# The down product of a feed-forward block by Strassen-Winograd instead of directly, in an attention and feed-forward kernel on one core

## Chip, core and metric

One of the eight cores of a Trainium2 chip. The metric is device time in microseconds of one execution, the median of several. The kernel is written with one program per engine and semaphores between them: TensorE (matmuls), VectorE, ScalarE, GpSimd, and SyncE, which issues every DMA. Each program runs in its written order.

## What is computed

`x` has 2 x 512 tokens of 1024 features. Three layers (a quantized product, a stream mixer, a cross-attention) come first; they are not touched. The last layer is a feed-forward block with low-rank corrections:

```python
gate = x @ gate_w.T + (x @ gate_a.T) @ gate_b.T      # 1024 -> 2752, rank 16
up   = x @ up_w.T   + (x @ up_a.T) @ up_b.T
hidden = silu(gate) * up
out = hidden @ down_w.T + (hidden @ down_a.T) @ down_b.T   # 2752 -> 1024
x = x + out
```

## The kernel before

Every float32 matrix is held as a float16 high half and a float16 low half (value minus high half), and a product is three matmuls: high x high, high x low, low x high. Splitting costs one ScalarE operation (the high half, a copy) and one VectorE operation (the low half, a subtraction). Weights are staged in four slots `STAGE` of 128 x 1024 float32; TensorE forms the rank-16 correction of a weight block in PSUM ("fold", contraction over 96 partitions), and VectorE adds it to the staged weights.

**Up stage.** Hidden features go in 21 slabs of 128 (`j` = 0 to 20) and a tail of 64 (`TAIL` = 21). Gate and up weights of a slab, and the tokens in two halves, form a 2 x 2 block matrix product that is already done by Strassen-Winograd: seven products A11, A12, S1, S2, S4, S3, A22 (`BLOCKS`) of 4 contraction tiles x 3 = 12 matmuls of 128x512 each. `form` makes S1 to S4 of the staged weights, `block_hi` and `block_lo` split them into a ring of 12 blocks (`SLAB`), `product` (line 2518 issues its matmuls) runs in the order of `products(j)`: S1, S2, S4 of slab j, A11 of j+1, S3 of j, A12 of j+1, A22 of j. `gate_second`, `up_second`, `gate_first` and `keep_*` combine the products; `hidden_second` and `hidden_first` multiply silu(gate) by up for the two token halves; `hidden_hi` and `hidden_rest` split the result into `HIDT` (hidden features x tokens). Some buffers of one slab lie in the place of a later slab of `HIDT` (`kept`, `silu_of`).

SyncE loads slab weights one by one (line 547): each load waits until the low half that last reads its slot is written. VectorE's loop over `j` (lines 2104 to 2137) and ScalarE's (lines 1294 to 1310) are written out by hand; both do slab j's sums, slab j+1's blocks and the first blocks of slab j+2.

**Down stage.** Output features are eight rows `m` of 128. For each m, `down` takes all 21 full hidden tiles x 2 token halves x 3 matmuls (`mm3`, lines 2170 to 2172), and two matmuls for the tail tile (lines 2574, 2575), into `PAIR[m % 2]`. The weights of a row come in pieces of 8, 8, 5 and half a hidden tile (`PIECES`), each folded (`down_fold`, line 2550), added (`down_add`, 1759) and split (`down_hi`, `down_lo`) into one of two buffers `DWN`, a row ahead. The residual x, of which four tiles were spilled to `x_keep` in the up stage, is read back, split into halves (`residual_hi`, `residual_lo`), transposed by DMA and summed into `OUT` (`residual_sum`); `finish` adds the scaled product (line 1789), and `send` stores it. Last, `out_t` (transposed) leaves with 2 KB rows.

Of the kernel before, what the change touches and what calls it, by code (L numbers as in the profile page):

```python
# [5 lines left out]
P = 128  # L6
B, S, D = 2, 512, 1024
# [45 lines left out]
N_LOADS = N_DOWN + KD * NP  # L53
ZEROED = 8 + N_DOWN - N_DF
# [37 lines left out]
def products(j):  # L92
# [7 lines left out]
         + [(TAIL, "L3"), (TAIL, "L4")])  # L100
# [45 lines left out]
def build(nc, x, ctx, ctx_t, consts, small_w, w_branch, wq, wk, bqk, gate_w, up_w, tail_w,  # L146
          down_w, down_tail, gate_a, gate_bt, up_a, up_bt, down_a, down_bt, out_t, x_keep):
    stack = ExitStack()
    with stack:
# [50 lines left out]
        DWN = [SLAB[:, at * KB:at * KB + 2 * HT * P].rearrange("p (s k c) -> p s k c", s=2, k=HT) for at in (0, 13)]  # L200
        XR = XT[:, :, :, :, :].rearrange("p b s k t -> p (b s k t)").rearrange("p (g s d) -> p g s d", g=NT, s=2)
# [5 lines left out]
        XD = X[:, :, :].rearrange("p g d -> p (g d)").bitcast(F16).rearrange("p (s m t) -> p s m t", m=KD, s=2)  # L207
# [54 lines left out]
        DA, DB = LORA[:, D:D + HID], LORA[:, 0:D]  # L262
# [8 lines left out]
        def factors_of(g, si, sj):  # L271
# [26 lines left out]
        out_done, spilled, xd_ok = [sem("out_even"), sem("out_odd")], sem("spilled"), sem("xd_ok")  # L298
# [14 lines left out]
        fac_ok, s_add, comb, b_lo, d_add, d_lo, xr_lo, out_v = (  # L313
            sem(n) for n in ("fac_ok", "s_add", "comb", "b_lo", "d_add", "d_lo", "xr_lo", "out_v"))
# [11 lines left out]
        b_hi, sg_ok, hid_hi, p1_ok, p5_ok, p6_ok, d_hi, xr_hi = (  # L326
            sem(n) for n in ("b_hi", "sg_ok", "hid_hi", "p1_ok", "p5_ok", "p6_ok", "d_hi", "xr_hi"))
# [8 lines left out]
        fold_p, mul_p, dfold_p, down_p = (sem(n) for n in ("fold_p", "mul_p", "dfold_p", "down_p"))  # L336
# [101 lines left out]
        def block_source(j, name):  # L438

            st = [STAGE[(N_SLAB + 2 * j + i) % SLOTS].rearrange("p (h k c) -> p h k c", h=2, k=KD // 2)
                  for i in range(2)]
            a11, a12, a21, a22 = (st[i][:, h] for i in range(2) for h in range(2))
            if j == TAIL:
                return {"K1": (a11, 0, None, NS), "K2": (a12, 1, None, NS)}[name]
            s1 = ST[:, :].rearrange("p (k c) -> p k c", k=KD // 2)
            return {"A11": (a11, 0, None, 2 * j + 1), "A12": (a12, 1, None, 2 * j + 1), "A22": (a22, 1, None, 2 * j + 2),
                    "A21": (a21, 0, None, 2 * j + 2), "S1": (s1, 0, 1, 4 * j + 1), "S2": (s1, 0, 1, 4 * j + 2),
                    "S4": (a12, 0, 1, 4 * j + 3), "S3": (a21, 0, 1, 4 * j + 4)}[name]

        def down_pair(m):
            return PAIR[m % 2]
# [4 lines left out]
        def _(e):  # L457
# [45 lines left out]
            def send(m):  # L503
                for h in range(B):
                    hs = slice(h * HALF, (h + 1) * HALF)
                    e.wait_ge(out_v, B * m + h + 1)
                    e.dma_start(out_t[m * P:(m + 1) * P, hs], OUT[:, m % 2, hs]).then_inc(out_done[m % 2], 16)
# [31 lines left out]
            for n in range(NS):  # L539
# [16 lines left out]
                elif n == SLOTS + 1:  # L556
# [8 lines left out]
            for m in range(KD):  # L565
                for i, (k0, k1) in enumerate(PIECES):
                    at, p_ = N_DOWN + m * NP + i, m * NP + i
                    if p_ < SLOTS:
                        e.wait_ge(fac_ok, 8 + 4 + p_ - SLOTS + 1)
                    else:  # L570
                        e.wait_ge(d_lo, p_ - SLOTS + 1)
                    kp = HTAIL if k1 == HT else P
                    st = STAGE[at % SLOTS][0:kp, 0:(k1 - k0) * P].rearrange("p (k c) -> p k c", k=k1 - k0)
                    e.dma_start(st, down_tail[m] if k1 == HT else down_w[m][:, k0:k1, :]).then_inc(
                        stg_in[at % SLOTS], 16)
                if m == 0:
                    e.wait_ge(mul_p, len(ORDER))
                    e.wait_ge(spilled, 16 * BT)
                    for g in range(BT):
                        e.dma_start(X[:, g, :], x_keep[g * P:(g + 1) * P, :]).then_inc(x_in[g], 16)  # L580
                if m in (1, 2):
# [2215 lines left out]
```

## Time and profile before

| | us |
|---|---|
| median of 3 runs | 1168.9 (1167.17 to 1169.38) |
| the profiled execution, its own time | 1169.75 |
| its span in the profile | 1167.9 |
| up stage, about | 503 to 929 |
| down stage, first to last matmul | 929.3 to 1164.5 |
| TensorE busy | 1103.2 |
| VectorE busy | 797.3 |
| ScalarE busy | 484.6 |

PE is TensorE (PEld its weight loads), DVE VectorE, ACT ScalarE, SP SyncE (SPq its queue of DMA issues), POOL GpSimd. A line of the timeline gives start, duration, engine, line, operation, output<-input and how many of them run on; in brackets the idle time before it and what ended it.
### The profile page before, as it was taken

Reading aid. Unit: us, or ns where it says so; the run is one execution under the profiler, and the core shown is the slowest. Engines: PE = TensorE matmul, PEld = TensorE weight load, DVE = VectorE, ACT = ScalarE, POOL = GpSimd, SP = SyncE. Lnnn points to the kernel's source line nnn. Section 1 sums busy time; section 2 is a strip of 40 time slices with the busy share of each in tenths; the row PEclk is TensorE's granted clock in tenths of the full one; section 3 lists DMA queues with packets and bytes.
Section 4 is the critical chain, followed back from the end, with each engine's and each line's share of the span. In section 5 each row is a group of like instructions: output and inputs, shape, how many; then the busy total and the mean of one; then the engine's idle time right before and its main releaser. Section 6 shows DMA issues by size and latency. Waiting matters only on the chain.

```text
span 1167.9 us, 16025 instructions
## 1 busy us (share of the span) xinstructions
PE 1103.2 (94%) x6144; PEld 540.9 (46%) x6150; DVE 797.3 (68%) x1600; ACT 484.6 (41%) x731; POOL 154.2 (13%) x184
## 2 busy tenths in 40 slices
PE   4786999899999999969999999999999999999998
PEld 2343554654445444424444444444444444444443
DVE  8999988889994177877767676767766664333330
ACT  6896652873145134744343434434343341111110
POOL 4883350073004010000000000000001000000000
PEclk9997999999999999999999999999999999999999
DMA  9620000223032029864111212020111375322200
GB/s 367 270 97 1 2 1 1 73 69 112 1 108 86 1 60 248 194 131 93 71 57 53 72 38 72 37 73 36 73 37 39 89 198 120 111 66 68 65 14 25
DMA packets 80061, 97.19 MB, mean 83 GB/s; under 512 B 57776, under 2 KB 58416, under 8 KB 79984
## 3 DMA queue, kind: packets, MB, share of 16 engines
q1 hardware_dynamic: 79984, 96.16, 27.0%
q8 instruction: 49, 0.80, 0.3%
q14 instruction: 28, 0.23, 0.1%
HBM read 76.22 MB, written 6.29 MB: 71 GB/s over the span
## 4 chain that ended last, share of the span: by engine, by line
PE 76%; DVE 18%; ACT 3%; issue 2%; DMA 1%; SPq 0%; DVEq 0%; ACTq 0%
PE PAIR L2518 32%; PE PAIR L2170 13%; PE PAIR L2171 12%; PE PAIR L2172 12%; DVE X L1558 2%; DVE PAIR L1510 2%; PE PAIR L2473 2%; DVE LORA L1509 1%; DVE LORA L1511 1%; DVE POOL L1384 1%; PE PAIR L2550 1%; DVE BST L1356 1%; DVE BST L1357 1%; DVE X L1427 1%; DVE XT L1421 1%
## 5 line engine op out<-in xcount | busy, mean ns | idle before, releaser
L2170 PE MATMUL PAIR<-POOL 128*128 128x512 f16 x672 | 255.8, 381 | 2.3 <-DVE POOL L1601 2.3
L2171 PE MATMUL PAIR<-POOL 128*128 128x512 f16 x672 | 255.8, 381 | 0.0
L2172 PE MATMUL PAIR<-POOL 128*128 128x512 f16 x672 | 255.7, 381 | 0.0
L2518 PE MATMUL PAIR<-XT,POOL 128*128 128x512 f16 x1008 | 230.2, 382 | 10.6 <-DMA XT<-POOL 6.9
L2518 PEld LDWEIGHTS PAIR<-XT,POOL 128*128 128x128 f16 x1008 | 98.2, 98 | 127.1 <-issue 14.0
L2518 PE MATMUL PAIR<-X,POOL 128*128 128x512 f16 x504 | 115.7, 379 | 0.4 <-DMA X<-POOL 0.4
L2172 PEld LDWEIGHTS PAIR<-POOL 128*128 128x128 f16 x672 | 65.8, 98 | 80.3 <-issue 1.4
L2170 PEld LDWEIGHTS PAIR<-POOL 128*128 128x128 f16 x672 | 65.6, 98 | 69.3 <-DVE POOL L1601 4.3
L2171 PEld LDWEIGHTS PAIR<-POOL 128*128 128x128 f16 x672 | 65.7, 98 | 65.5 <-issue 0.6
L1064 ACT ACTIVATE POOL<-STG 128x1024 f16<-128x1024 f32 (+2 forms) x32 | 25.3, 790 | 169.7 <-DVE STG L1759 169.7
L1759 DVE SCALAR_TENSOR_TENSOR STG<-STG,PAIR 128x1024 f32<-128x1024 f32 (+2 forms) x32 | 28.3, 884 | 89.8 <-PE PAIR L2550 86.7
L667 POOL MEMSET STG<- 96x1024 f32 (+1 forms) x12 | 11.0, 923 | 522.5 <-DVE POOL L1691 475.7
L2518 PEld LDWEIGHTS PAIR<-X,POOL 128*128 128x128 f16 x504 | 48.4, 98 | 55.9 <-issue 1.1
L1691 DVE TENSOR_TENSOR POOL<-STG,POOL 128x512 f16<-128x512 f32 x107 | 69.7, 684 | 0.7 <-ACT POOL L996 0.7
L996 ACT ACTIVATE POOL<-STG 128x512 f16<-128x512 f32 x107 | 62.0, 621 | 3.7 <-DVE STG L1671 3.6
L1704 DVE TENSOR_TENSOR POOL<-POOL,PAIR 128x512 f32<-128x512 f32 x21 | 14.4, 688 | 71.4 <-PE PAIR L2518 71.4
L996 ACT ACTIVATE POOL<-ST 128x512 f16<-128x512 f32 x42 | 26.3, 626 | 80.6 <-DVE ST L1686 80.6
L2518 PE MATMUL PAIR<-T4B,POOL 128*128 128x512 f16 x252 | 57.8, 379 | 1.2 <-issue 1.2
L1671 DVE SCALAR_TENSOR_TENSOR STG<-STG,PAIR 128x1024 f32<-128x1024 f32 x43 | 52.1, 1214 | 0.0
L1510 DVE RECIPROCAL PAIR<-LORA 128x16 f32<-128x16 f32 (+1 forms) x168 | 46.8, 279 | 5.8
L2170 PE MATMUL PAIR<-XT,POOL 128*128 128x512 f16 x128 | 48.5, 379 | 1.2 <-ACT XT L906 1.2
L2172 PE MATMUL PAIR<-XT,POOL 128*128 128x512 f16 x128 | 48.5, 379 | 0.0
(305 smaller groups left out, 1707.9 us busy)
## 6 DMA issues: line engine op xcount, KB each, us to landing
STG<-in_gate_w SPq DMA_DIRECT2D x21, 512.0 KB, 3.5
STG<-in_up_w SPq DMA_DIRECT2D x21, 512.0 KB, 4.3
STG<-in_ctx_t SPq DMA_DIRECT2D x16, 512.0 KB, 3.8
STG<-in_ctx SPq DMA_DIRECT2D x16, 512.0 KB, 4.2
STG<-in_down_w SPq DMA_DIRECT2D x16, 512.0 KB, 3.6
POOL<-in_ctx SPq DMA_DIRECT2D x12, 512.0 KB, 11.1
X<-in_x SPq DMA_DIRECT2D x8, 512.0 KB, 9.7
out_t<-T4B SPq DMA_DIRECT2D x16, 256.0 KB, 2.0
```

The source lines that it names most:

```text
L996: e.activation(block(j, name)[:, 0, :, :], src, ACT.Copy).then_inc(b_hi, 1)
L1064: last = e.activation(DWN[(m + 1) % 2][0:kp, 0, k0:k1, :], st, ACT.Copy)
L1510: chain(e.reciprocal(rr, rs))
L1558: i = e.scalar_tensor_tensor(xs, H[:, g, sj * CST:(sj + 1) * CST], factors_of(g, si, sj), xs, ALU.mult, ALU.add)
L1671: e.scalar_tensor_tensor(st, st, WS, PAIR[aux.pair("fold", n)][:, :], ALU.mult, ALU.add).then_inc(s_add, 1)
L1691: e.tensor_tensor(blk[:, 1, :, :], block_source(j, name)[0], blk[:, 0, :, :], ALU.subtract).then_inc(b_lo, 1)
L1759: e.scalar_tensor_tensor(st, st, WS, PAIR[aux.pair("dfold", m, i)][0:kp, 0:w_], ALU.mult, ALU.add).then_inc(d_add, 1)
L2170: e.matmul(dst, l_hi, r_hi, start=first, stop=False)
L2171: e.matmul(dst, l_hi, r_lo, start=False, stop=False)
L2172: return e.matmul(dst, l_lo, r_hi, start=False, stop=last)
L2473: i = e.matmul(PAIR[pr][:, k * P + c0:k * P + c0 + w], fa[0:GRP * 32, k * P:(k + 1) * P], fb[0:GRP * 32, j * P:j * P + w], start=True, sto ...
L2518: i = e.matmul(dst, blk[:, a_, k, :], src[:, b_, k, :], start=(opens and k == 0 and n == 0), stop=(k == KD // 2 - 1 and n == 2), skip_grou ...
```

## The change

The down product is done by Strassen-Winograd as well. Output rows are taken in pairs (`p` = 0 to 3, two rows of 128), hidden tiles in pairs (`i` = 0 to 10, the eleventh with the tail), tokens in halves. The pairs of hidden tiles are worked through in three sets of 4, 4 and 3 (`SETS`), so there are 12 chunks `d` = 3p + c; chunk d counts as slab `j = HT + d` and uses the ring, `form`, `block_hi` and `block_lo` of the up stage. The seven products of a pair p accumulate in seven banks over its three chunks; the eighth bank is `bank_f` for folds.

On the hidden side three more operands are made for each pair of hidden tiles, in the up stage: sums of the two token halves of two neighbouring slabs ("turns": `turn_first`, `turn_middle` (2 operations), `turn_last` on VectorE), each split by `turn_hi` (ScalarE) and `turn_lo` (VectorE). For pairs 0 to 7 the three split operands are parked in DRAM (`t_keep`, `park`), and come back in five DMAs of 6 MB in all where the down stage begins (`back_in`). VectorE's `turn_lo` stands behind `up_second` of each even slab from 2 on.

The residual's splitting, transposing (`turn_residual`) and storing to `xt_keep` (`keep_residual`: two DMAs with pieces of 256 bytes) is moved from the down stage into slabs 2, 3, 4, 5, 7, 9, 11 and 13 of the up stage; `load_sum` reads 256 KB pieces back. `evacuate` on VectorE (13 operations) and `first_product` on ScalarE combine the seven banks with the residual into `OUT`.

Core of the diff:

```diff
+ACCS = 13
+SETS = ((0, 4), (4, 8), (8, HT // 2))
+NSET = len(SETS)
+CHUNKS = NSET * KD // 2
...
+RESIDUAL = ((2, 4), (3, 5), (4, 6), (5, 7), (7, 0), (9, 1), (11, 2), (13, 3))
+PARKED = 8
...
@@ SyncE, behind the load of slab weights n (j = n // 2)
+                if n % 2 and j - 2 in R_AT:
+                    turn_residual(R_AT[j - 2])
+                    keep_residual(R_AT[j - 2])
+                if n % 2 and 4 <= j and j % 2 == 0 and j // 2 - 2 < PARKED:
+                    park(j // 2 - 2)
+                if n % 2 and j in R_AT and R_AT[j] >= 4:
+                    load_residual(R_AT[j])
...
@@ SyncE, the down stage; load_sum(p, 2) and (p, 3) wait for residual_sum(p, 0) and (p, 1)
+            load_down(0)
+            load_down(1)
+            e.wait_ge(mul_p, DONE[TAIL - 1, "S3"])
...
+            for p in range(KD // 2):
+                load_sum(p, 0)
+                load_sum(p, 1)
+                for d in range(NSET * p + 2, min(NSET * p + 5, CHUNKS)):
+                    load_down(2 * d)
+                    load_down(2 * d + 1)
+                    if d == NSET * p + 2:
+                        load_sum(p, 2)
+                        load_sum(p, 3)
+                send(p)
...
@@ ScalarE
             def hidden_hi(j):
                 e.wait_ge(hid_v, 2 * j + 2)
+                if j % 2:
+                    e.activation(HIDT[:, j, 0, HALF:D], kept(j), ACT.Copy).then_inc(hid_hi, 1)
+                    e.wait_ge(t_v, 2 * j + 2)
+                else:
+                    e.wait_ge(t_v, 2 * j + 1)
+                    e.activation(HIDT[:, j, 0, HALF:D], made_in(j // 2, HELD2), ACT.Copy).then_inc(hid_hi, 1)
...
+            def first_product(p):
+                e.wait_ge(mul_p, DONE[HT + NSET * p + NSET - 1, "A11"])
...
+                e.activation(out_part(1, 0), bank_d["A11"], ACT.Copy, scale=1.0 / (HS * WS)).then_inc(first_ok, 1)
...
                 silu(j)
                 if 1 <= j < TAIL - 1:
                     keep_first(j + 1)
+                if j and j % 2 == 0:
+                    for kind in (HELD3, HELD2, HELD4):
+                        turn_hi(j // 2 - 1, kind)
...
+            for d in range(1, CHUNKS + 1):
+                if d < CHUNKS:
+                    for name in BLOCKS:
+                        block_hi(HT + d, name)
+                if d % NSET == 0:
+                    first_product(d // NSET - 1)
...
@@ VectorE, loop over slabs
                 if j:
                     hidden_first(j - 1)
+                    if j % 2:
+                        turn_first(j - 1)
+                    else:
+                        turn_last(j - 1)
...
                 if j + 2 <= TAIL:
                     slab_add(2 * j + 4)
+                if j in R_AT:
+                    residual_lo(R_AT[j])
                 up_second(j)
+                if j and j % 2 == 0:
+                    for kind in (HELD3, HELD2, HELD4):
+                        turn_lo(j // 2 - 1, kind)
                 if j + 2 < TAIL:
                     slab_add(2 * j + 5)
                 hidden_second(j)
+                if j % 2:
+                    turn_middle(j)
...
@@ VectorE, the down stage
+            for d in range(1, CHUNKS + 1):
+                if d < CHUNKS:
+                    j = HT + d
+                    down_add(j, 0)
+                    down_add(j, 1)
+                    block_lo(j, "A11")
+                    down_add(j, 2)
+                    down_add(j, 3)
+                    form(j, "S1")
+                    block_lo(j, "A12")
+                    block_lo(j, "S1")
+                    for name in ("S2", "S4", "S3"):
+                        form(j, name)
+                    for name in ("S2", "S4", "S3", "A22"):
+                        block_lo(j, name)
+                if d % NSET == NSET - 1:
+                    residual_sum(d // NSET, 0)
+                    residual_sum(d // NSET, 1)
+                elif d % NSET == 0:
+                    evacuate(d // NSET - 1)
...
@@ TensorE; fold (j, i) waits for add (j, i - 1), all in bank_f
+            def down_product(j, name):
...
+                if name == "A11":
+                    if p and c == 0:
+                        e.wait_ge(first_ok, p)
...
+                elif name == "A12":
+                    if p and c == 0:
+                        e.wait_ge(acc_v, at + 1)
...
-                    if name == "L2":
-                        down_fold(0, 0)
-            down_fold(0, 1)
+                    if j == TAIL - 1 and name in ("S3", "L2", "A22"):
+                        down_fold(HT, ("S3", "L2", "A22").index(name))
             tail_product("L3")
+            down_fold(HT, 3)
             tail_product("L4")
+            for j in range(HT, HT + CHUNKS):
+                first = 3 if j == HT else 2
+                for n, name in enumerate(BLOCKS):
+                    down_product(j, name)
+                    if j + 1 < HT + CHUNKS and first <= n < first + 4:
+                        down_fold(j + 1, n - first)
```

In the start of the down stage VectorE does, in this order: the add of fold 0, a memset and the last factor piece, the add of fold 1, low halves of A11 and A12, `hidden_first` and `turn_first` of slab 20, the add of fold 2, the first tail product, `hidden_rest`, the add of fold 3, the forms and low halves of chunk 0, and, between them, the rest of the tail and its three turns with their low halves. The tail's hidden tile is now split in full (its other 64 partitions are zero), so its pair takes three matmuls like the others.

## Rows read from the trace of the kernel before

**Rows 1.** The page: busy time by engine, and the chain by line.
```profile
PE 1103.2 (94%) x6144; PEld 540.9 (46%) x6150; DVE 797.3 (68%) x1600; ACT 484.6 (41%) x731; POOL 154.2 (13%) x184
...
PE PAIR L2518 32%; PE PAIR L2170 13%; PE PAIR L2171 12%; PE PAIR L2172 12%; DVE X L1558 2%; DVE PAIR L1510 2%; PE PAIR L2473 2%; DVE LORA L1509 1%; DVE LORA L1511 1%; DVE POOL L1384 1%; PE PAIR L2550 1%; DVE BST L1356 1%; DVE BST L1357 1%; DVE X L1427 1%; DVE XT L1421 1%
```

**Rows 2.** Windows, one of the up stage, one of the down stage; columns in the profile section.
```profile
700.00:860.00 160.00, 160.00 (x843) 76.63 (x842) 110.41 (x165) 65.36 (x111) 0.00 (x0) 1.00 0.16 55
1000.00:1060.00 60.00, 60.00 (x314) 28.39 (x312) 19.61 (x23) 6.93 (x10) 0.00 (x0) 1.00 0.21 67
```

**Rows 3.** Timeline where the down stage begins: start us, us, engine, line, operation.
```profile
917.07 2.75 PE L2538 MATMUL PAIR<-XT,POOL 128*128 128x512 f16 x12
...
920.60 0.61 PE L2550 MATMUL PAIR<-LORA 96*128 96x128 f16 x8 [0.78 <-DVE LORA L1663]
...
921.05 2.75 PE L2518 MATMUL PAIR<-T4B,POOL 128*128 128x512 f16 x12
921.32 1.22 DVE L1759 SCALAR_TENSOR_TENSOR STG<-STG,PAIR 128x1024 f32<-128x1024 f32 x1 [0.86 <-PE PAIR L2550]
...
929.27 0.38 PE L2170 MATMUL PAIR<-POOL 128*128 128x512 f16 x1
```

**Rows 4.** Timeline of the end.
```profile
1164.33 0.38 PE L2575 MATMUL PAIR<-POOL 128*128 128x512 f16 x1
1164.75 0.69 DVE L1789 SCALAR_TENSOR_TENSOR T4B<-PAIR,T4B 128x512 f32<-128x512 f32 x1 [13.27 <-PE PAIR L2575]
```

**Rows 5.** Timeline of one up slab, some 19 us.
```profile
861.51 0.69 DVE L1709 TENSOR_TENSOR POOL<-POOL,PAIR 128x512 f32<-128x512 f32 x1 [2.15 <-PE PAIR L2518]
...
863.25 0.68 DVE L1714 SCALAR_TENSOR_TENSOR POOL<-POOL 128x512 f32<-128x512 f32 x1
...
867.46 0.68 DVE L1686 TENSOR_TENSOR ST<-ST,STG 128x512 f32<-128x512 f32 x1
...
868.17 0.69 DVE L1686 TENSOR_TENSOR STG<-STG,ST 128x512 f32<-128x512 f32 x1
...
869.28 0.60 ACT L1009 ACTIVATE POOL<-PAIR 128x512 f32<-128x512 f32 x1 [0.58 <-PE PAIR L2518]
...
872.57 5.34 PE L2518 MATMUL PAIR<-XT,POOL 128*128 128x512 f16 x24
...
875.36 0.69 DVE L1704 TENSOR_TENSOR POOL<-POOL,PAIR 128x512 f32<-128x512 f32 x1 [3.49 <-PE PAIR L2518]
...
876.68 0.33 SPq L547 DMA_DIRECT2D STG<-in_tail_w  x1
877.17 1.22 DVE L1671 SCALAR_TENSOR_TENSOR STG<-STG,PAIR 128x1024 f32<-128x1024 f32 x1
...
882.28 0.69 DVE L1714 SCALAR_TENSOR_TENSOR POOL<-POOL 128x512 f32<-128x512 f32 x1
```

**Rows 6.** DMA issues: count, KB each, median us from issue to landing.
```profile
STG<-in_gate_w SPq DMA_DIRECT2D x21, 512.0 KB, 3.5
STG<-in_up_w SPq DMA_DIRECT2D x21, 512.0 KB, 4.3
...
X<-XT SPq DMA_TRANSPOSE x8, 5.0
LORA<-in_small_w SPq DMA_DIRECT2D x1, 96.0 KB, 6.2
```

**Rows 7.** The page: costliest groups, ScalarE's high halves.
```profile
L996 ACT ACTIVATE POOL<-ST 128x512 f16<-128x512 f32 x42 | 26.3, 626 | 80.6 <-DVE ST L1686 80.6
```

**Rows 8.** TensorE's timeline: the products behind its two long idles.
```profile
515.28 2.75 PE L2518 MATMUL PAIR<-XT,POOL 128*128 128x512 f16 x12 [3.74 <-DVE POOL L1698]
...
525.79 5.08 PE L2518 MATMUL PAIR<-XT,POOL 128*128 128x512 f16 x12 [6.87 <-DMA XT<-POOL]
```

**Rows 9.** Windows in and behind the second of these idles; PEclk third from the end.
```profile
521.00:524.00 3.00, 0.00 (x0) 0.00 (x0) 3.00 (x6) 2.08 (x5) 0.00 (x0) 0.95 1.05 197
524.00:527.00 3.00, 1.21 (x3) 0.44 (x4) 2.91 (x6) 1.10 (x3) 0.00 (x0) 0.50 0.93 177
```

More of the change, by code:

```diff
@@ L593, in _ @@
+            for n in range(2):
+                e.wait_ge(out_done[n], 16 * KD)
         @prog.gpsimd
@@ L1008, in keep_fifth @@
                 e.wait_ge(mul_p, DONE[j, "S1"])
+                if j == 10:
+                    for n in range(2):
+                        e.wait_ge(parked[n], LANDED + (32, 16)[n])
+                elif j == 14:
+                    for n in range(2):
+                        e.wait_ge(r_kept[n], LANDED + 16 * len(RESIDUAL))
                 e.activation(kept(j), bank_c, ACT.Copy).then_inc(p5_ok, 1)
@@ new lines, in residual_hi @@
+            def residual_hi(i):
+                g = RESIDUAL[i][1]
+                if i >= 2:
+                    e.wait_ge(r_turned[i % 2], LANDED + 16 * (i // 2))
+                if g < BT:
+                    e.wait_ge(r_in[i % 2], LANDED + 16 * (i // 2 - 1))
+                else:
+                    e.wait_ge(x3_ok, g + 1)
+                if i == 0:
+                    for t in range(BT):
+                        for group in range(3):
+                            wait_turned(e, t, group)
+                e.activation(RH[i % 2][:, 0:D], X[:, g, :] if g >= BT else RESX[i % 2], ACT.Copy).then_inc(r_hi, 1)
@@ L2116, in _ @@
                     factor(N_DF, DB, 2, WS)
+                    factor(N_DF + 1, DA[:, 0:HID], 1, 1.0, 0, 1)
                 gate_second(j)
@@ L2155, in _ @@
-            for i in range(NP):
-                down_add(1, i)
-                down_lo(1, i)
-            for m in range(KD):
-                if m != 1 and m < KD - 1:
-                    for i in range(NP):
-                        down_add(m + 1 if m else 2, i)
-                        down_lo(m + 1 if m else 2, i)
-                residual_sum(m)
-                finish(m)
+            tail_rest(0)
+            block_lo(HT, "S3")
+            block_lo(HT, "A22")
+            tail_turn(HELD3)
@@ L2540, in tail_product @@
                 i.then_inc(mul_p, 1)
-            def down_fold(m, i):
-                k0, k1 = PIECES[i]
-                pr = aux.pair("dfold", m, i)
-                aux.wait_empty(e, "dfold", m, i)
-                if m == 0 and i == 0:
-                    e.wait_ge(fac_ok, 12)
-                kp = HTAIL if k1 == HT else P
-                for k in range(k0, k1):
-                    last = e.matmul(PAIR[pr][0:kp, (k - k0) * P:(k - k0 + 1) * P], DA[0:GRP * 32, k * P:k * P + kp],
-                                    DB[0:GRP * 32, m * P:(m + 1) * P], start=True, stop=True)
-                last.then_inc(dfold_p, 1)
@@ L2781 @@
         "tail_w": up_tiles(tail)[0],
-        "down_w": dw[:, :full].reshape(KD, P, HT - 1, P).transpose(0, 3, 2, 1),
-        "down_tail": dw[:, full:].reshape(KD, P, 1, HTAIL).transpose(0, 3, 2, 1),
+        "down_w": down_tiles[:, :, [2 * i + h for a0, a1 in SETS for h in range(2) for i in range(a0, a1)], :],
         "gate_a": a["L1_ffn_gate_a"], "gate_bt": a["L1_ffn_gate_b"].T,
```

550 lines of the change are left out of this document (360 added, 190 removed).

## The prediction

> **What bounds the kernel now.** I read the page's totals and chain first: TensorE is busy 94% of the span, and the largest line of the chain that ended last is its up products, 32% [rows 1]. The windows then show where: in the up stage (700 to 860 us) and in the down stage (1000 to 1060 us) TensorE is busy all of the time at granted clock 1.00, VectorE 110.4 of 160 us and 19.6 of 60 us [rows 2]. So every matmul taken out of the down stage is worth its full slot as long as nothing new makes TensorE wait. The timeline gives the slots and the slack. Down stage: first matmul at 929.27, last at 1164.33 [rows 3, 4]. It issues 8 x 2 x (21 x 3 + 2) = 1040 matmuls and 160 fold matmuls (16 more lie before it). A product of 12 matmuls stands with 2.75 us, a single matmul with 0.38 [rows 3], so they start (2.75 - 0.38) / 11 = 0.2155 us apart and a product costs 2.59. Eight folds take 0.45 us (920.60 to 921.05) [rows 3]: 0.056 us each. 1040 x 0.2155 = 224.1 us; the other 11.2 us of the stage are folds.
>
> **The change, part by part.**
>
> *Matmuls.* Strassen takes 7 products x 11 hidden pairs x 3 matmuls x 4 pairs of output rows = 924. 116 fewer x 0.2155 = **-25.0 us**. Still 176 folds, in groups of 3 or 4 instead of 8, 5 and a lone one: 160 x 0.056 = 9.0 to the present 11.2; I take 10.2, **-1.0**.
>
> *Up stage.* Per two slabs VectorE gets 7 new operations of 512 columns, and in eight slabs a residual operation of 1024 (1.22 us, as the slab's add [rows 5]). Independent operations follow each other every 0.60 us, dependent ones every 0.71 (867.46 to 868.17). VectorE idles 3.49 us before the gate sum and 2.15 us before the up sum [rows 5]. Between up sum and gate sum lie at most four new ones (three low halves and the first turn: 2.5 us of 3.49), before the up sum at most the residual's (1.2 of 2.15). Both fit. ScalarE gets at most three high halves and one residual half a slab; its keep of the S1 product (869.28) moves to about 871.2, as it stands behind the hidden high half that now waits for a turn, and S4 starts at 872.57 [rows 5]: still 0.7 us early. Cost 0, bound 0 to 1 us a slab if that cover goes; next late would be S4.
>
> SyncE's queue is where the residual's steps block: transpose, wait for it, two stores, then a parked store, and only then the next slab's load. From the slab's add (time 0): residual low half ends 2.4; transpose lands 5.0 us later [rows 6]; the stores are issued by 8.9, if each takes twice the 0.33 us of a plain load's issue [rows 5], as they have more pieces (my estimate); the slab load goes out near 9.5 and is needed at 19.0, one period later (863.25 to 882.28 [rows 5]). Landing is 3.5 to 4.3 us plus 1.3 MB of stores ahead; inside. At slab 14 the keep of S1 also waits for the last residual store: needed by about 13.7, expected 13 to 14. **+0.3**, bounds 0 and 3.
>
> *Start of the down stage.* Fold 0 now stands before L2 and fold 1 after it; fold 1 waits for the add of fold 0, which stands behind three low halves and the last full slab's hidden product: 917.3 + 0.6 for the up sum + 4 x 0.6 + 0.7 gives 921.0, a stall of 1.2 us where 0.78 was [rows 3]. The other folds are met. Products then start at 929.6: **+0.3**. In chunk 0, the fold after S4 (942.8) needs the first add of chunk 1. VectorE has 32 operations before it (factor, blocks, tail, turns, their low halves), at 0.60 to 0.71 each and some 2 us of waits for ScalarE: to 944.4, add to 945.0: **+2.3**, bounds 0 and 5. The 6 MB of parked halves come back from 917 on; the first 2 MB are needed at 937, and half a megabyte lands in 3.5 to 4.3 us [rows 6], so they are in time.
>
> *Each new pair of rows* (three times: chunks 3, 6, 9). Two waits:
>
> (a) SyncE issues the weights of chunk 3p+3 behind the third and fourth residual loads, and these wait for VectorE's residual sums, which stand behind the whole preparation of chunk 3p+2. Let T be the start of A22 in chunk 3p+1. This chunk's operations have 384 columns: 1.22 us for 1024 and 0.68 for 512 columns [rows 5], continued, give 0.55. The chunk's last add starts at T+0.27 (921.05 to 921.32 [rows 3]); ten more at 0.47, or 0.58 where dependent, end near T+6.0 and the two sums at T+6.6 and T+7.2; the weights are issued at T+7.7 and land, by 3.5 to 4.3 us [rows 6] and half a megabyte ahead of them, at T+12.0. Add 0 ends T+12.7. TensorE reaches fold 1 at T+2.59+3 x 1.94+0.22+1.94 = T+10.6. Stall 2.2 us, bounds 1 and 3.5.
>
> (b) The first product of chunk 3p+3 overwrites the bank that ScalarE's first_product reads, and ScalarE does that behind all seven high halves of this chunk. With U the start of A22 (9 matmuls, 1.94 us): add 3 at U+0.27, S1 formed from U+0.98, its high half to U+2.3 (0.62 [rows 7]), low half to U+3.0, S2, S4, S3 formed at U+3.1, 3.8, 4.4, the high halves of S3 and A22 at U+5.1 and 5.7, first_product to U+6.8 (0.60, as the other bank reads on ScalarE [rows 5]). A11 starts U+6.9 instead of U+1.94: **5.0 us**, bounds 3.5 and 6.5. VectorE's thirteen evacuating operations (0.69 [rows 4]) then run to U+16.4; the bank waits and fold 1 (U+17.4) are behind that.
>
> Together 3 x 7.2 = **+21.6**.
>
> *The clock.* After 3.74 us of idle TensorE resumed at full clock; in the idle of 6.87 us the granted clock went from 1.00 to 0.50 (2.4 to 1.2 GHz) before it resumed at 525.79, and 12 matmuls took 5.08 instead of 2.75 us, **2.3 us** lost [rows 8, 9]. In the window 521 to 524 the mean is 0.95 [rows 9], so it fell about 4.8 us into that idle. My stall (b) is 5.0: between the two rows, at the edge. I take one fall in three, +2.3. The Trainium skill (TensorE: Matmul & The Clock Gate, "HAM oscillation") says that waits of some microseconds between groups of matmuls make every next group start cold; by it the sum would be +7.0 here instead of +2.3. The trace has one idle on each side, so it settles neither.
>
> *The end.* After S3 of the last chunk seven evacuating operations remain: 0.2 + 7 x 0.69 = 5.0 us after S3, which is 3.1 after the last matmul. Now it is 0.9 (1164.55 to 1165.44 [rows 4]): **+2.2**.
>
> *Sum*: -25.0 - 1.0 + 0.3 + 0.3 + 2.3 + 21.6 + 2.3 + 2.2 = **+3.0 us** on the profiled execution's 1169.75. That execution is 0.85 above the median of 1168.9, so I say **1172** for the median.
>
> **Rivals** (all against the median).
> 1. *The load of (a) is not late.* If the residual sums are reached, or the loads land, by T+8.7, (a) disappears, -6.6: 1165.3, faster. For it: the landing rows are medians of a queue that was idle, and VectorE is only lightly loaded. Against: it needs three microseconds less on a path of queued steps. It decides below 8.7 us from T to landing; 17%.
> 2. *The clock never falls.* 1169.7, within the noise; 3.74 us kept the clock [rows 8]. 20%. *It falls at all three* (3 x 2.3): 1176.7; 12%.
> 3. *Small stores.* The residual's stores are 2048 pieces of 256 bytes. A load of 1024 small pieces took 6.2 us [rows 6]. If two stores take 12 us, slab loads land some 3 to 7 us past their time in eight slabs, less a cover of about 2.5: some +14, 1186. Against: transposes of tiles as large land in 5.0 [rows 6]. The Trainium skill (DMA: Bandwidth & Descriptors, "Specifications") states that pieces under 512 bytes are written below line rate; no run here shows such a store. 11%.
> 4. That the change does less than it says, more matmuls or more slabs of wait: the counts follow from its loops; 2%.
>
> My forecast (one or two falls, both stalls): 38%.
>
> **How the numbers follow.** Forecast 1172, its own range 1169 to 1176. The range for 8 in 10 takes rival 1 and 2 and the bounds of the stalls (3 x 1.5 each way; below, chunk 0 by 2.3 and no clock fall; above, all three falls): 1163 to 1180. A measurement of this kernel can tell about 0.2% (2.3 us): faster is below 1166.6, slower above 1171.2. Faster: rival 1 and short stalls, 0.2. Same: rival 2's first half and a part of the forecast's lower side, 0.25. Slower: the rest, 0.55.
>
> **What would show it.** In the changed profile: 924 down matmuls; no idle of TensorE in the up stage; three idles near 5 us before the first products of chunks 3, 6 and 9, released by ScalarE's first_product, each preceded some 7 us earlier by one of about 2 us before a fold, released by VectorE's add and behind it by a load; windows with granted clock below 1.00 only just after the former; SyncE waiting for the residual sum. I am wrong if TensorE idles per pair sum to under 4 us, if idles stand in the up stage, or if the down stage is not shorter in busy time by 25 us.

## The result, and the profile after

The changed kernel takes 1188.66 us (median of 4 runs, 1186.33 to 1190.79) beside 1169.14 for the kernel before on the same chip: ratio 1.0169, interval 1.0147 to 1.0192, **1.7% slower**. The forecast was 1172 with a range of 1163 to 1180: the sign is right, the size is missed and lies outside the range. The profiled execution took 1188.8 us, 19.05 more than that of the kernel before, which is the sum that the steps below are held against.

The page of the changed kernel, its busy times, its chain by engine and by line, and two of its DMA issues:

```profile
PE 1091.5 (92%) x6028; PEld 535.5 (45%) x6034; DVE 917.0 (77%) x1830; ACT 523.9 (44%) x815; POOL 155.8 (13%) x183
...
PE 61%; DVE 28%; ACT 5%; DMA 3%; issue 3%; SPq 0%; DVEq 0%; ACTq 0%
PE PAIR L2789 31%; PE PAIR L2887 13%; PE PAIR L2441 4%; PE PAIR L2443 4%; PE PAIR L2442 4%; DVE PAIR L1686 3%; DVE LORA L1685 3%; DVE LORA L1687 3%; DVE X L1734 2%; DMA STG<-in_down_w 2%; PE PAIR L2744 2%; DVE POOL L1867 1%; DVE POOL L1560 1%; PE PAIR L2648 1%; DVE BST L1532 1%
...
STG<-in_down_w SPq DMA_DIRECT2D x16, 512.0 KB, 7.5
...
xt_keep<-POOL SPq DMA_DIRECT2D x16, 256.0 KB, 3.0
```

Against [rows 1], the load of the down weights is new on the chain, as 2% of the span. The windows say where to look (columns as in [rows 2]: length, busy time of PE, PEld, DVE, ACT and POOL, then granted clock, DMA share, GB/s):

```profile
700.00:860.00 160.00, 160.00 (x844) 76.64 (x842) 133.35 (x199) 73.59 (x127) 0.00 (x0) 1.00 0.34 104
...
940.00:1000.00 60.00, 48.15 (x235) 22.02 (x233) 33.80 (x57) 15.75 (x28) 0.00 (x0) 0.90 0.20 67
1000.00:1060.00 60.00, 53.71 (x269) 24.97 (x267) 30.95 (x51) 9.66 (x17) 0.00 (x0) 0.95 0.25 83
...
982.00:985.00 3.00, 2.33 (x9) 1.17 (x10) 1.90 (x3) 1.26 (x2) 0.00 (x0) 0.50 0.40 161
...
997.00:1000.00 3.00, 2.98 (x8) 1.07 (x9) 2.83 (x6) 0.00 (x0) 0.00 (x0) 0.50 0.04 14
```

In the up stage VectorE does 133.35 us of work in 160 where it did 110.4, and TensorE is still busy for all 160: the new operations there cost nothing. In the down stage, where TensorE was always busy at 1.00 [rows 2], it now idles 11.85 of 60 us and the clock averages 0.90. TensorE's timeline shows the pattern, which comes three times, at chunks 3, 6 and 9:

```profile
975.69 2.11 PE L2887 MATMUL PAIR<-X,POOL 128*128 128x512 f16 x9
982.67 0.61 PE L2821 MATMUL PAIR<-LORA 96*128 96x128 f16 x4 [4.87 <-DVE STG L1975]
983.07 4.05 PE L2887 MATMUL PAIR<-POOL 128*128 128x512 f16 x9
...
997.02 10.45 PE L2887 MATMUL PAIR<-POOL 128*128 128x512 f16 x36 [4.83 <-DVE POOL L1867]
```

Idle (a) is 4.87, 4.76 and 3.83 us, idle (b) 4.83 each time, and both do harm after their end too. Nine matmuls take 2.11 us at the full clock and 4.05 behind (a); 36 take 7.93 at the full clock and 10.45 behind (b). The two windows at 982 and 997 show 0.50, which is 1.2 of 2.4 GHz. What held each idle is seen on the other engines (timelines of VectorE, of SyncE's queue and of ScalarE, in order of time):

```profile
973.06 1.29 DVE L1989 TENSOR_TENSOR T4B<-LORA 128x512 f32<-128x512 f16 x2
973.77 1.19 SPq L627 DMA_DIRECT2D LORA<-xt_keep  x2
975.00 2.02 SPq L613 DMA_DIRECT2D STG<-in_down_w  x4
981.92 0.69 DVE L1975 SCALAR_TENSOR_TENSOR STG<-STG,PAIR 128x512 f32<-128x512 f32 x1 [7.58 <-DMA STG<-in_down_w]
...
995.73 1.89 DVE L1867 TENSOR_TENSOR POOL<-STG,POOL 128x512 f16<-128x512 f32 x3
...
996.30 0.58 ACT L1215 ACTIVATE T4B<-PAIR 128x512 f32<-128x512 f32 x1
```

For (a) the chain runs as forecast: residual sums, two residual loads, weights, add, fold. But the weights, issued at 975.00, are there only at 981.9, 6.9 us later. For (b) the profile names VectorE's low half (L1867) as the last releaser. ScalarE's reading of the bank (L1215) ends at 996.88 though, and A11 starts at 997.02; two causes are possible, and only an experiment tells them apart. Last, VectorE at the end, in place of the 0.9 us after the last matmul of [rows 4]:

```profile
1179.44 1.29 DVE L1998 SCALAR_TENSOR_TENSOR T4B<-PAIR,T4B 128x512 f32<-128x512 f32 x2 [0.53 <-PE PAIR L2887]
1180.83 2.94 DVE L2001 TENSOR_TENSOR T4B<-T4B,LORA 128x512 f32<-128x512 f32 x4
1183.81 0.69 DVE L1998 SCALAR_TENSOR_TENSOR T4B<-PAIR,T4B 128x512 f32<-128x512 f32 x1
```

### The profile page after: what moved, and what is told of

It reads as the page before. It is cut to its first block, busy times and chain, and to the rows that moved or that the text cites. A ratio compares the mean times of both kernels' runs of the same rounds, so it can differ in the third digit from the quotient of the medians.

```text
span 1187.0 us, 16323 instructions
## 1 busy us (share of the span) xinstructions
PE 1091.5 (92%) x6028; PEld 535.5 (45%) x6034; DVE 917.0 (77%) x1830; ACT 523.9 (44%) x815; POOL 155.8 (13%) x183
## 4 chain that ended last, share of the span: by engine, by line
PE 61%; DVE 28%; ACT 5%; DMA 3%; issue 3%; SPq 0%; DVEq 0%; ACTq 0%
PE PAIR L2789 31%; PE PAIR L2887 13%; PE PAIR L2441 4%; PE PAIR L2443 4%; PE PAIR L2442 4%; DVE PAIR L1686 3%; DVE LORA L1685 3%; DVE LORA L1687 3%; DVE X L1734 2%; DMA STG<-in_down_w 2%; PE PAIR L2744 2%; DVE POOL L1867 1%; DVE POOL L1560 1%; PE PAIR L2648 1%; DVE BST L1532 1%
## 5 line engine op out<-in xcount | busy, mean ns | idle before, releaser
L2789 PE MATMUL PAIR<-XT,POOL 128*128 128x512 f16 x1008 | 230.9, 382 | 9.0 <-DMA XT<-POOL 5.3
L1129 ACT ACTIVATE POOL<-STG 128x512 f16<-128x512 f32 (+1 forms) x167 | 96.2, 612 | 108.7 <-DVE STG L1975 104.0
L2887 PE MATMUL PAIR<-POOL 128*128 128x512 f16 x528 | 128.5, 403 | 14.5 <-DVE POOL L1867 14.5
L2441 PE MATMUL PAIR<-POOL 128*128 128x512 f16 x336 | 128.1, 381 | 2.3 <-DVE POOL L1777 2.3
L2442 PE MATMUL PAIR<-POOL 128*128 128x512 f16 x336 | 128.0, 381 | 0.0
L2443 PE MATMUL PAIR<-POOL 128*128 128x512 f16 x336 | 128.0, 381 | 0.0
L1129 ACT ACTIVATE POOL<-ST 128x512 f16<-128x512 f32 (+1 forms) x64 | 39.5, 617 | 166.5 <-DVE ST L1862 166.5
L1867 DVE TENSOR_TENSOR POOL<-STG,POOL 128x512 f16<-128x512 f32 (+1 forms) x167 | 106.2, 669 | 1.2 <-ACT POOL L1129 1.1
L1975 DVE SCALAR_TENSOR_TENSOR STG<-STG,PAIR 128x512 f32<-128x512 f32 (+1 forms) x48 | 30.8, 642 | 94.5 <-PE PAIR L2821 72.9
L2887 PEld LDWEIGHTS PAIR<-POOL 128*128 128x128 f16 x528 | 53.7, 103 | 82.2 <-DVE POOL L1867 15.9
L2443 PEld LDWEIGHTS PAIR<-POOL 128*128 128x128 f16 x336 | 32.9, 98 | 40.4 <-issue 1.1
L2441 PE MATMUL PAIR<-XT,POOL 128*128 128x512 f16 x128 | 48.5, 379 | 1.2 <-ACT XT L1039 1.2
L2442 PE MATMUL PAIR<-XT,POOL 128*128 128x512 f16 x128 | 48.5, 379 | 0.0
L2443 PE MATMUL PAIR<-XT,POOL 128*128 128x512 f16 x128 | 48.5, 379 | 0.0
L2441 PEld LDWEIGHTS PAIR<-POOL 128*128 128x128 f16 x336 | 32.8, 98 | 33.0 <-DVE POOL L1777 4.4
```

Of the source, the lines that this page charges most:

```text
L1129: e.activation(block(j, name)[:, 0, :, :], src, ACT.Copy).then_inc(b_hi, 1)
L1867: e.tensor_tensor(blk[:, 1, :, :], block_source(j, name)[0], blk[:, 0, :, :], ALU.subtract).then_inc(b_lo, 1)
L1975: e.scalar_tensor_tensor(st, st, WS, bank_f[:, 0:depth(j) * P], ALU.mult, ALU.add).then_inc(s_add, 1)
L2441: e.matmul(dst, l_hi, r_hi, start=first, stop=False)
L2442: e.matmul(dst, l_hi, r_lo, start=False, stop=False)
L2443: return e.matmul(dst, l_lo, r_hi, start=False, stop=last)
```

## The experiments

**Theory.** The loss is six idles, each worth itself and the slow stretch behind it; (a) comes from the order on SyncE's queue, (b) from the place of first_product on ScalarE. **Rivals**: (b) waits for VectorE's low halves; the weights are late because other loads run beside them; the slow clock is a matter of the whole stage and does not go with the idles. Times of the experiments are given as ratios to the kernel before on the same chip; a difference in us between two kernels is the difference of their ratios times 1168.

**1. Weights before the residual loads.**

```diff
 for d in range(NSET * p + 2, min(NSET * p + 5, CHUNKS)):
     load_down(2 * d)
     load_down(2 * d + 1)
-    if d == NSET * p + 2:
+    if d == min(NSET * p + 3, CHUNKS - 1):
         load_sum(p, 2)
         load_sum(p, 3)
```

> The third and fourth residual loads of a row pair are issued behind the weights of chunk 3p+3 instead of ahead of them. Theory (each idle of TensorE costs itself and then some 2 us of half clock): the idles before the second fold of that group (4.9, 4.8 and 3.8 us) are gone, and with them the slow stretch behind each (together 6.4 us): 1188.7 - 13.5 - 6.4 = about 1169. Rival (the half clock comes from the density of the work as a whole, not from these idles): only the 13.5 us of idle go, about 1175, and the granted clock stays below 1.00 in the same places. Second rival (the weights are late for their own sake): no change, 1188.

Measured: 1168.76 us, ratio 1.0017 (1.0005 to 1.0030), 17.8 less than the changed kernel. (a) is gone, (b) stands unchanged. SyncE's queue and TensorE:

```profile
959.61 1.53 SPq L613 DMA_DIRECT2D STG<-in_down_w  x2
...
991.58 9.23 PE L2887 MATMUL PAIR<-POOL 128*128 128x512 f16 x36 [4.83 <-DVE POOL L1867]
```

The weights go out at 959.6 instead of 975.0. The three idles were 13.46 us and the slow stretches behind them 6.0, together 19.4; the intervals allow 14.8 to 20.8. A move of two loads takes back most of what the change lost.

**2. first_product early, and the evacuation in parts.** ScalarE reads the bank right after the high half of A12 instead of after all seven; VectorE's first two evacuating operations (one frees the bank of A12, the other uses first_product's result) come after the low half of A11, the next two after the third add, the rest where it was.

```diff
@@ ScalarE
-                if d % NSET == 0:
+                        if d % NSET == 0 and name == "A12":
+                            first_product(d // NSET - 1)
+                elif d % NSET == 0:
...
@@ VectorE, in the loop over the chunks
+                    if d % NSET == 0:
+                        evacuate(d // NSET - 1, 0)
...
+                    if d % NSET == 0:
+                        evacuate(d // NSET - 1, 1)
...
-                    evacuate(d // NSET - 1)
+                    evacuate(d // NSET - 1, 2 if d < CHUNKS else None)
```

> ScalarE's first_product runs behind the high half of A12 instead of behind all seven, and VectorE's first four evacuating operations run between the adds of chunk 3p+3. Theory: the three idles of 4.83 us before A11 of chunks 3, 6 and 9 go, and the slow stretch behind each (together 6.4 us): 1188.7 - 14.5 - 6.4 = about 1168; the idles before the second fold stay. Rival (clock not bound to the idles): about 1174. Second rival (A11 waits for its weight block's low halves, as the profile's releaser has it, not for the bank): no change.

Measured: 1177.68 us, ratio 1.0078 (1.0052 to 1.0104), 10.6 less than the changed kernel. (b) is gone, 36 matmuls take 7.93 us again. (a) is 5.02, 5.13 and 4.50, and a new idle of 1.79 us appears three times, before fold 1 of the next chunk:

```profile
1005.41 0.40 PE L2831 MATMUL PAIR<-LORA 96*128 96x128 f16 x4 [1.79 <-DVE STG L1977]
```

The add that it needs stands behind the rest of the evacuation. So 14.5 us of idle and some 5.9 of slow stretches went, and 6.5 of idle and 1.5 of slow stretch behind (a) came: 12.4 us by the rows, where the ratios give 10.6. The expected 1168 was missed by 10 us mostly because the expectation had no wait handed on.

**3. Both.** The diffs of 1 and 2 together.

> Both edits together. Theory: no idle of over 2.2 us is left in the down stage, granted clock 1.00 from 1000 us on: 1188.7 - 28 - 12.8 = about 1148, below the kernel before by about 1.8%. Rival (clock not bound to the idles): about 1161. If either edit only hands its wait on, the time lies near the better of the two single ones, 1168.

Measured: 1154.24 us, ratio 0.9886 (0.9868 to 0.9905), **faster than both kernels**, and 33.1 less than the changed one, where 1 and 2 alone gave 28.4; the intervals, about 3 us to each side, leave room for a plain sum. Of the idles remain the 2.15 of chunk 0 and three of 1.96 before fold 1 of chunks 4, 7 and 10. These 5.9 us are the larger part of what the expected 1148 lacked. TensorE's timeline, and a window of the down stage:

```profile
996.59 0.40 PE L2831 MATMUL PAIR<-LORA 96*128 96x128 f16 x4 [1.96 <-DVE STG L1977]
...
1000.00:1060.00 60.00, 58.04 (x306) 27.52 (x304) 39.89 (x65) 13.16 (x23) 0.00 (x0) 1.00 0.29 97
```

With the long idles the slow clock went too (1.00 in the window): it belongs to them, not to the stage. Behind the idles of 1.96 us the matmuls run at full speed; behind the 2.15 of chunk 0 they did not this time (last section).

**4. The idle (b) filled.** The waits stay, but TensorE does 20 matmuls that nobody uses before A11 of chunks 3, 6 and 9.

```diff
+                    if n == 0 and j > HT and (j - HT) % NSET == 0:
+                        e.wait_ge(s_add, NS + 4 * (j - HT) + 4)
+                        for _ in range(20):
+                            e.matmul(bank_f, HIDT[:, 0, 0, 0:P], HIDT[:, 0, 0, 0:HALF], start=True, stop=True)
```

> Nothing is taken out: before A11 of chunks 3, 6 and 9, where TensorE idles 4.83 us, it issues 20 matmuls into the fold bank that nobody reads (20 x 0.2155 = 4.3 us). Theory: the granted clock holds behind these three, the others stay slow: 1188.7 - 6.4 = about 1182. But if the clock is already low from the idle before the second fold, the filling itself runs partly at half clock and the gain is 1 to 2 us less. Rival (clock not bound to idles): 1189 or more.

Measured: 1183.87 us, ratio 1.0144 (1.0118 to 1.0170). TensorE's timeline:

```profile
980.77 0.52 PE L2821 MATMUL PAIR<-LORA 96*128 96x128 f16 x4 [4.34 <-DVE STG L1975]
981.08 3.71 PE L2887 MATMUL PAIR<-POOL 128*128 128x512 f16 x9
...
988.96 4.48 PE L3059 MATMUL PAIR<-POOL 128*128 128x512 f16 x20
993.96 7.93 PE L2887 MATMUL PAIR<-POOL 128*128 128x512 f16 x36 [0.52 <-DVE POOL L1867]
```

A11 still waits for the same work, yet its 36 matmuls take 7.93 us where 10.45 were. The slow stretch comes from the idle, not from the work behind it. The time shows less: 2.9 us by the ratios, 4.8 by the medians, for the 5.9 us of slow stretches; with intervals of some 3 us to each side this run alone prices nothing, and the rows carry the verdict.

**5. first_product early, nothing else.** Only the ScalarE part of the diff of 2.

> Only ScalarE's order: first_product behind the high half of A12. Theory (A11 waits for the bank that first_product frees): the idles of 4.83 us before A11 of chunks 3, 6 and 9 go, and one before A12 takes their place, since VectorE's first evacuating operation still stands behind the whole preparation: 0.7 to 8.1 us against A11's end at 4.5 us from the start of A22, so 3.6 us. Time 1188.7 - 3 x 1.2, and up to 2 us less for each of the three where the shorter idle leaves the clock alone: 1179 to 1185. Rival (A11 waits for low halves of its weights): no change, 1188.

Measured: 1184.08 us, ratio 1.0140 (1.0123 to 1.0157). TensorE's timeline:

```profile
989.73 2.75 PE L2889 MATMUL PAIR<-POOL 128*128 128x512 f16 x12
996.07 7.02 PE L2889 MATMUL PAIR<-POOL 128*128 128x512 f16 x24 [3.59 <-DVE T4B L2000]
...
1109.11 0.61 PE L2823 MATMUL PAIR<-LORA 96*128 96x128 f16 x4 [2.99 <-DVE STG L1977]
1109.51 3.41 PE L2889 MATMUL PAIR<-POOL 128*128 128x512 f16 x9
```

A11 now starts at once, though VectorE's low halves, which the profile had named as its releaser, are where they were. So first_product was the cause, and the rival falls. The idle moves to A12, whose bank waits for the evacuation at its old place (L2000), 3.59 us. That is why experiment 2 needed both halves. Its idles are 4.8 us shorter in all, the slow stretches as long as before, and it gains 3.4.

**6. The load behind the late one held back.** The weights of chunk 3p+4, issued right behind those of 3p+3, wait for the first add of 3p+3.

```diff
                 if d < 2:
...
+                if d > 3 and d % NSET == 1 and i == 0:
+                    e.wait_ge(s_add, NS + 4 * (d - 1) + 1)
```

> The weights of chunk 3p+4, which are issued at once behind those of chunk 3p+3, are held back until add 0 of chunk 3p+3 is done; nothing else is moved. Theory (the weights of 3p+3 land in 6.9 us instead of the 4.3 that the rows of before have, because four loads and two residual loads share the DMA engines): landing about 4.5 us, the idle before the second fold 2 to 2.5 us instead of 4.9, 4.8 and 3.8, no clock fall there: 1188.7 - 3 x 2.2 - 6.4 = about 1176. Rival (the landing is slow because of the two residual loads ahead of it): idle and time as they were, 1187 to 1189.

Measured: 1187.69 us, ratio 1.0181 (1.0154 to 1.0209), no gain. SyncE's queue and VectorE's add:

```profile
975.22 7.36 SPq L615 DMA_DIRECT2D STG<-in_down_w  x4
...
981.01 0.69 DVE L1977 SCALAR_TENSOR_TENSOR STG<-STG,PAIR 128x512 f32<-128x512 f32 x1 [6.46 <-DMA STG<-in_down_w]
```

Without the next chunk's loads behind them the weights still take 5.8, 6.4 and 6.3 us to land, where 6.9, 6.8 and 5.9 were; (a) is 3.75, 4.40 and 4.26, together 12.4 us where 13.5 were.

**7. The wait kept, the loads turned round.** The weights of chunk 3p+3 still wait for the residual sums, but the two residual loads are issued behind them. That parts the wait from what stands ahead in the queue.

```diff
+                    if d == NSET * p + 3:
+                        e.wait_ge(sum_v, 2 * p + 2)
...
-                    if d == NSET * p + 2:
+                    if d == min(NSET * p + 3, CHUNKS - 1):
```

> The wait for VectorE's residual sums stays in front of the weights of chunk 3p+3, but the two residual loads are issued behind these weights instead of ahead. Theory (the weights land late because of the residual loads ahead of them in the DMA engines): issue 0.6 us earlier, landing 4.3 instead of 6.9 us, the idle before the second fold near 2 us instead of 4.9, no clock fall there: 1188.7 - 3 x 2.5 - 6.4 = about 1175. Rival (whatever is in flight shares the engines, in whichever order): landing 6 us or more, idle above 3.5 us, 1184 to 1188.

Measured: 1173.55 us, ratio 1.0042 (1.0022 to 1.0062). SyncE's queue, VectorE's add and TensorE:

```profile
974.42 0.81 SPq L613 DMA_DIRECT2D STG<-in_down_w  x2
975.27 1.18 SPq L627 DMA_DIRECT2D LORA<-xt_keep  x2
...
977.95 0.69 DVE L1977 SCALAR_TENSOR_TENSOR STG<-STG,PAIR 128x512 f32<-128x512 f32 x1 [3.55 <-DMA STG<-in_down_w]
...
978.69 0.40 PE L2823 MATMUL PAIR<-LORA 96*128 96x128 f16 x4 [0.84 <-DVE STG L1977]
...
990.20 10.18 PE L2889 MATMUL PAIR<-POOL 128*128 128x512 f16 x36 [4.83 <-DVE POOL L1869]
```

Issued only 0.6 us earlier, the weights are there in 3.5, 4.6 and 3.7 us instead of 6.9, 6.8 and 5.9. (a) shrinks to 0.84, 1.93 and 1.06, none of them with a slow stretch behind it. So 2.2 to 3.4 us of each landing came from the two residual loads ahead in the queue.

**8. Both of the last two.** The same, with the load behind held back as well.

> As e9_sums_behind, and the weights of chunk 3p+4 held back until the first add of chunk 3p+3, so that the first weights have only their pair and the residual loads behind them in flight. Theory of shared engines: landing near 3.6 to 4.3 us as in the kernel before, idle 1.5 to 2 us, 1174. If e9 is slow and this is fast, it is the load in flight; if both are fast, it is what is queued ahead; if both are slow, the load is slow for a reason of its own (the half of a row it reads).

Measured: 1175.49 us, ratio 1.0053 (1.0034 to 1.0073); the weights land in 3.6, 4.1 and 3.6 us, and (a) is 0.91, 1.43, 0.96. The intervals of 7 and 8 overlap: no effect of the loads behind is seen.

**9. The last idles.** Experiment 3, with the first add of chunk 1 ahead of the last turn of the tail, and the first adds of chunks 4, 7 and 10 between the eighth and ninth operation of the evacuation.

```diff
@@ before the last tail_turn
+            down_add(HT + 1, 0)
...
-                    down_add(j, 0)
+                    if d != 1 and d % NSET != 1:
+                        down_add(j, 0)
...
@@ evacuate
+                if part == 2:
+                    down_add(j + 2, 0)
```

> On top of e3_both: VectorE does the first add of chunk 1 before the last turn of the tail, and the first add of chunks 4, 7 and 10 between the eighth and ninth evacuating operation. Theory: the idle of 2.15 us in chunk 0 and the three of 1.96 us before the second fold of chunks 3, 6 and 9 go: 1154.2 - 2.1 - 5.9 = about 1146. Rival (the adds only hand the wait on to the products that wait for the evacuation or the turns, A22): 1152 to 1154, with idles before A22.

Measured: 1146.49 us, ratio 0.9815 (0.9794 to 0.9837), 8.3 us less than 3 for 8.0 us of idle. Windows:

```profile
940.00:1000.00 60.00, 60.00 (x321) 28.90 (x320) 44.54 (x73) 17.76 (x31) 0.00 (x0) 1.00 0.28 91
1000.00:1060.00 60.00, 60.00 (x315) 28.63 (x314) 43.15 (x71) 15.54 (x27) 0.00 (x0) 1.00 0.30 99
```

The down stage now runs from 931.76 to 1140.29 without an idle: 208.5 us where 235.3 were [rows 3, 4]. This is what the algorithm itself is worth, 26.8 us.

**10. The end.** Experiment 9, with the last pair's four residual additions ahead of the operations that use S3.

```diff
+                if p == KD // 2 - 1:
+                    add_residual(o21, 3, 1, 4)
...
+                    add_residual(o22, 2, 0, 8)
+                    e.wait_ge(acc_v, at + 10)
+                    scaled(o21, "S3", o21)
+                    scaled(o22, "S3", o22)
+                    e.wait_ge(acc_v, at + 12)
+                    scaled(o21, "A22", o21)
+                    return
```

> On top of e7_adds_early: in the last row pair the four additions of the residual stand before the operations that wait for S3, where VectorE idled 3 us in all. The last seven operations behind S3 become three, but the chain before them is VectorE's own by then: I expect the end 1.2 us earlier, about 1145. Rival (the residual's last two loads, issued 10 us before, land too late for it): no gain, or a loss of up to 1 us.

Measured: 1144.22 us, ratio 0.9797 (0.9775 to 0.9818), **the best version: 2.0% faster than the kernel before**. VectorE's timeline at the end; TensorE's last matmul ends at 1135.1:

```profile
1133.93 1.42 DVE L2004 TENSOR_TENSOR T4B<-T4B,LORA 128x512 f32<-128x512 f32 x2
1135.38 2.02 DVE L2001 SCALAR_TENSOR_TENSOR T4B<-PAIR,T4B 128x512 f32<-128x512 f32 x3
```

VectorE ends 2.3 us after the last matmul instead of 3.4. The gain on 9 is 2.1 us by the ratios, but the intervals of 9 and 10 overlap, so the rows show it and the times don't prove it.

## Why the prediction was wrong in size

The waits and their places were forecast; the sizes of two terms were not. Its terms beside what the profiles show (us, on the profiled executions) are in the table. The row on the layers ahead of the change is not its work: over the twelve profiles here the same product of the first slab starts anywhere from 511.4 to 516.7 us.

| step | forecast | measured | from |
|---|---|---|---|
| matmuls and folds | -26.0 | -26.8 | experiment 9: 208.5 for 235.3 |
| up stage and start of down stage | +0.6 | +1.2 | from the first up product (503.61, now 502.58) to the first down matmul (929.27, now 929.46) |
| layers ahead of the change | 0 | -1.0 | first up product at 502.58 for 503.61 |
| chunk 0 | +2.3 | +2.15 | idle before the fold |
| (a), three times | +6.6 | +13.5 | 4.87 + 4.76 + 3.83 |
| (b), three times | +15.0 | +14.5 | 3 x 4.83 |
| clock | +2.3 | +13.0 | stage of 251.65, less 30.10 of idle, less 208.53 (see below) |
| end | +2.2 | +2.5 | 3.4 us after the last matmul for 0.9 |
| sum | +3.0 | +19.05 | profiled executions: +19.05 |

**Two steps failed.** The larger is **the clock**, which took "one fall in three", and for (b) alone. All six idles were followed by half clock: 2.8, 1.5 and 1.7 us lost behind (a), 2.5, 1.7 and 1.7 behind (b), each against the same records at full speed. That is 11.9 of the 13.0. The other 1.2 us are seven idles at 0.17 each, as an idle is counted from a modelled end (nine matmuls stand with 2.11 us, and the next thing starts 1.94 after them).

The step read one idle on each side, 3.74 kept and 6.87 lost, as the two ends of a scale, and put 5.0 at its edge. That was too much to rest on two rows, and "one idle on each side" was not all that the trace of before held. In an earlier layer stand two idles of 2.1 and 2.3 us; the granted clock is 1.00 in the window 86 to 89, ahead of the first, and in 107 to 109.3, which is the second itself:

```profile
91.87 1.46 PE L2277 MATMUL PAIR<-LORA,XT 128*128 128x24 f16 x48 [2.13 <-ACT LORA L788]
...
109.31 0.38 PE L2170 MATMUL PAIR<-XT 128*128 128x512 f16 x1 [2.26 <-DVE XT L1545]
...
91.80:94.00 2.20, 1.46 (x48) 1.36 (x48) 2.20 (x1) 0.01 (x1) 2.20 (x5) 0.50 0.00 0
...
109.30:112.00 2.70, 2.69 (x27) 1.52 (x28) 2.45 (x9) 2.70 (x6) 0.00 (x0) 0.76 0.00 0
```

Behind the first the clock stood at 0.50, behind the second it averaged 0.76. So an idle shorter than the 3.74 could be followed by the lower clock, and a scale by length alone did not fit the trace. TensorE does small matmuls around both, so the rows do not show that the idles alone did it. The (a) idles were left out of the step because they were forecast at 2.2 us, so the first error hung on the second. The rule of the Trainium skill (TensorE: Matmul & The Clock Gate, "HAM oscillation"), that waits of some microseconds make every next group of matmuls start cold, was weighed there and given the smaller share; the rows agree with it for every idle of the changed down stage but the 2.15 us of chunk 0. The measurement puts it ahead of the step's reading. Applied to (b) alone, as the text did, it too would have given only +7.0.

The second is **(a)**: "land, by 3.5 to 4.3 us and half a megabyte ahead of them, at T+12.0". T+7.7 and 4.3 is T+12.0, so the half megabyte was priced at what lies between the two rows. These are the gate weights, with nothing ahead (3.5), and the up weights, each issued 0.6 us behind gate weights of the same size (4.3); rival 1 calls both "medians of a queue that was idle", which holds for the first alone. SyncE's queue before:

```profile
648.31 0.33 SPq L547 DMA_DIRECT2D STG<-in_gate_w  x1
648.91 0.50 SPq L547 DMA_DIRECT2D STG<-in_up_w  x1
```

So half a megabyte of weights ahead cost 0.8 us. The two residual loads, as much in all and issued 1.2 us before, cost 2.2 to 3.4: the weights took 6.9, 6.8 and 5.9 us. Experiment 7 shows the residual loads as the cause, and experiments 6 and 8 show no more than a small part of the loads behind. Why they cost more than weights ahead is not shown; they move in packets of 1 KB where the weights have 4 KB, and no run changes that. The issue itself, the sums and the fold came as forecast: the sums end at 974.35 and the weights are issued at 975.00, 0.65 later. (a) was bounded at 3.5; all three lie above it.

**What held**: the count (the trace has 924 matmuls and 160 folds from the first down matmul on, as forecast), the slots, a free up stage with 23 us more of VectorE work in 160, both mechanisms and their places, (b) to 0.2 us and first_product as its releaser against what the profile named, the end. Rival 1 (the load not late) is false by 3.8 to 4.9 us a pair, and it would have been near true with the order of experiment 7. Rival 2 is false at both ends: its upper one, three falls at 1176.7, counted half of the six. Rival 3 is false: the stores of 256-byte pieces landed in 3.0 us, 1.0 more than the output's stores of the same size in 2 KB pieces (2.0), and TensorE waited for none of them. Its 6.2 us was no price of small pieces: that load, at the very start (3.1 to 9.3 us), shared DMA engines that were busy 98.6% of the time and moved 2.4 MB.

What the algorithm is worth, 26.8 us, was forecast as 26.0; experiment 10 brings home 23.7 of it (1 - 0.9797, by 1168) with the same arithmetic.

## What to carry to other kernels

Price an idle of TensorE as itself plus the matmuls behind it at half clock: here 1.3 to 3.0 us more for nearly every idle of 3 us and up, and often for one of 2 to 3. Look through the whole trace for idles and what followed them, not only near the change. When a load is costed from a median landing time, look at what its queue issues just ahead, in the row and in the new place: half a megabyte ahead cost 0.8 us in one case and 2.2 to 3.4 in the other. And when an algorithm that does less work comes out slower, look first at the order of the queues: here moving two loads, one bank read and the operations that use it turned 1.7% slower into 1.1% faster.

## What was not expected of the hardware

The same idle at the same place is followed by the full clock in one profile and by half clock in another. The one that the forecast leant on is the clearest: in the kernel before, 12 matmuls behind an idle of 3.74 us took 2.75 us [rows 8]. That idle, 3.73 or 3.74 us, is in the profiles of the changed kernel and of all ten experiments, and there they took 4.11 to 5.28 us each time. The row was the one exception in twelve. At the short side it is the other way round. The idle of chunk 0, 2.14 to 2.16 us, stands in nine profiles; behind seven of them 12 matmuls took 2.75 us, and behind two, those of experiments 3 and 8, over 4. The changed kernel, for both idles:

```profile
514.25 4.32 PE L2789 MATMUL PAIR<-XT,POOL 128*128 128x512 f16 x12 [3.74 <-DVE POOL L1874]
...
944.95 0.40 PE L2821 MATMUL PAIR<-LORA 96*128 96x128 f16 x4 [2.15 <-DVE STG L1975]
945.19 2.75 PE L2887 MATMUL PAIR<-X,POOL 128*128 128x512 f16 x12
```

Experiment 3, for the second:

```profile
943.01 0.40 PE L2831 MATMUL PAIR<-LORA 96*128 96x128 f16 x4 [2.15 <-DVE STG L1977]
943.25 4.27 PE L2897 MATMUL PAIR<-X,POOL 128*128 128x512 f16 x12
```

Far ahead of the change, two short idles that all twelve profiles share go either way as well: behind one of 2.42 us, 32 matmuls took 3.84 us in two profiles and 5.22 to 6.78 in ten; behind one of 2.94, eight took 1.09 or 1.10 in four and 1.59 to 1.97 in eight. Behind a third, of 2.41 to 2.48 us at 214 to 215 us in six profiles, the matmuls kept the full clock each time. In the down stages all idles of 2.99 us and more were followed by slow matmuls, and none of the twelve of 0.84 to 1.96. So in these kernels the length of an idle sets a chance, not a yes or no. What decides within it stays open. The depth differs too: behind equal idles of 4.83 us, 36 matmuls lost 2.5, 1.7 and 1.7 us in the changed kernel and 1.3, 2.7 and 1.7 in experiment 1.
